# A maximum over 1024 keys in one VectorE instruction: two matmuls in a row, two banks freed together

## What is computed

```python
def attention(x, ctx, wq, wk, wv, wo, bo):        # self-attention: ctx is x
    q = x @ wq; k = ctx @ wk; v = ctx @ wv        # 16 heads of 64
    sim = einsum('bhid,bhjd->bhij', q, k) * 64 ** -0.5     # 1024 x 1024 per head
    attn = softmax(sim)
    return einsum('bhij,bhjd->bhid', attn, v) @ wo + bo
```

## Time and profile before

| | |
|---|---|
| median of 3 runs | 2324.59 us (2319.39 to 2327.59) |
| the profiled execution | 2328.06 us, its span 2326.3 us |
| TensorE busy | 2142.8 us, 92% |
| VectorE busy | 1743.6 us, 75% |
| ScalarE busy | 1476.1 us, 63% |
| GpSimd busy | 1155.2 us, 50% |

### The profile page before, as it was taken

The page is one execution under the profiler, slowest core; times in us unless marked ns, Lnnn a source line. Parts: engine busy times, 40 slices in busy tenths (PEclk is TensorE's granted clock), DMA queues, the critical chain, the costliest instruction groups (busy, mean ns, idle before and its releaser), DMA issues.

```text
span 2326.3 us, 59157 instructions
## 1 busy us (share of the span) xinstructions
PE 2142.8 (92%) x25392; PEld 1434.0 (62%) x25392; DVE 1743.6 (75%) x3148; ACT 1476.1 (63%) x1948; POOL 1155.2 (50%) x730
## 2 busy tenths in 40 slices
PE   4999999999899999989989999998998999999899
PEld 1566666675556666667556666666755666667675
DVE  5888888557588888755768888866576888886664
ACT  2788788345388888823547887773353888786342
POOL 3666665233076766622326766652223667664231
PEclk8999999999999999999999999999999999999999
DMA  3222221000132222001032222100103223210000
GB/s 107 71 73 52 61 62 38 10 31 23 51 105 52 58 74 63 18 10 38 24 83 73 52 75 77 43 27 1 38 23 81 70 61 83 61 36 20 10 11 19
DMA packets 60165, 114.19 MB, mean 49 GB/s; under 512 B 9344, under 2 KB 21632, under 8 KB 59904
## 3 DMA queue, kind: packets, MB, share of 16 engines
q1 hardware_dynamic: 59904, 110.41, 17.5%
HBM read 55.72 MB, written 4.19 MB: 26 GB/s over the span
## 4 chain that ended last, share of the span: by engine, by line
PE 65%; DVE 21%; ACT 9%; issue 3%; DMA 1%; POOL 1%; SPq 0%; POOLq 0%; DVEq 0%; ACTq 0%
PE scores L861 7%; DVE minima L1411 7%; PE scores L854 7%; PE work L831 7%; PE scores L746 6%; PE scores L748 6%; PE scores L747 6%; DVE prob L1426 4%; PE work L746 4%; PE work L747 4%; PE work L748 4%; PE work L883 3%; PE work L879 3%; PE work L881 3%; ACT prob L1214 3%
## 5 line engine op out<-in xcount | busy, mean ns | idle before, releaser
L693 POOL TENSOR_TENSOR prob<-prob 128x1024 f16<-128x1024 f32 x256 | 584.7, 2284 | 556.0 <-ACT prob L1215 545.2
L1411 DVE TENSOR_REDUCE minima<-work 128x1 f32<-128x512 f32 x1024 | 680.2, 684 | 43.0 <-PE work L831 29.4
L1214 ACT ACTIVATE prob<-scores 128x1024 f32<-128x1024 f32 x512 | 525.6, 1026 | 129.2 <-PE scores L861 112.0
L1215 ACT ACTIVATE prob<-scores 128x1024 f16<-128x1024 f32 x512 | 523.3, 1022 | 0.0
L883 PE MATMUL work<-vals,prob 128*128 128x65 f16 x4096 | 429.6, 196 | 0.0
L881 PE MATMUL work<-vals,prob 128*128 128x64 f16 x4096 | 429.4, 193 | 0.0
L879 PE MATMUL work<-vals,prob 128*128 128x65 f16 x4096 | 429.0, 193 | 0.4
L879 PEld LDWEIGHTS work<-vals,prob 128*128 128x128 f16 x4096 | 383.1, 99 | 62.1 <-issue 3.1
L881 PEld LDWEIGHTS work<-vals,prob 128*128 128x128 f16 x4096 | 379.9, 97 | 58.2
L831 PE MATMUL work<-ka,qa 128*128 128x512 f16 x1024 | 390.5, 386 | 24.0 <-DVE minima L1411 18.2
L883 PEld LDWEIGHTS work<-vals,prob 128*128 128x128 f16 x4096 | 380.3, 97 | 0.0
(11 more groups left out here) (160 smaller groups left out, 4179.0 us busy)
## 6 DMA issues: line engine op xcount, KB each, us to landing
qa<-staged_q SPq DMA_DIRECT2D x128, 128.0 KB, 2.3
ka<-staged_k SPq DMA_DIRECT2D x128, 128.0 KB, 2.3
raw_even<-in_pairs SPq DMA_DIRECT2D x32, 384.0 KB, 3.3
raw_odd<-in_pairs SPq DMA_DIRECT2D x32, 384.0 KB, 3.3
raw_odd<-in_pieces SPq DMA_DIRECT2D x20, 512.0 KB, 3.7
raw_even<-in_pieces SPq DMA_DIRECT2D x20, 512.0 KB, 3.6
qb<-staged_q SPq DMA_DIRECT2D x64, 128.0 KB, 2.3
kb<-staged_k SPq DMA_DIRECT2D x64, 128.0 KB, 2.3
```

The source lines that it names most:

```text
L693: pool.tensor_tensor(prob[1][:, slot, :], prob32[:, slot, :], prob[0][:, slot, :], ALU.subtract).then_inc(a.polished, 1)
L1214: act.activation(prob32[:, n % RING, :], source, ACT.Exp)
L1215: act.activation(prob[0][:, n % RING, :], source, ACT.Exp)\
L1411: dve.tensor_reduce(minima[:, t, h:h + 1], out[:, :], AX.X, ALU.max, negate=True)\
```

## The change

Both halves' matmuls of a tile stand in a row, into two neighbouring banks that are now one tile `peaks` of 1024 columns. One VectorE instruction reads all 1024 and writes the negated maximum, as float16, straight into the tile's column of `shift16`. The `combine` step, the tile `minima` and the semaphore `shift_combined` are gone. Both banks are filled and freed together, so the ring has one place: the next tile's first matmul waits until the read of this tile is over. `shift` writes into the same place, so it waits for tile 7's read, and the maximum behind it waits for the copy of `shift`. In the step list the maximum is now one entry, ahead of what is placed and of `score`.

```diff
-SCORE_RING, PEAK_RING, HIGH_RING = 2, 2, 1
+SCORE_RING, PEAK_RING, HIGH_RING = 2, 1, 1
...
-    tiles = [[Step("max", (t, h), par, head, 0) for h in range(BLKS)] for t in range(TILES)]
+    tiles = [[Step("max", t, par, head, 0)] for t in range(TILES)]
...
-    tiles[-1] = tiles[-1] + [Step("combine", 0, par, head, 0)]
...
-        out += [step for step in peaks_of[s] if step.kind == "arrive"] + peaks[:1]
+        out += peaks_of[s]
         out += placed[s]
         out.append(Step("score", s, par, head, 0))
         out += [take(step) for step in placed[s] if step.kind in HIGH]
-        out += peaks[1:] + [step for step in peaks_of[s] if step.kind == "combine"]
...
-        work = [ps(f"work{i}", BLK) for i in range(4)]
+        peaks = ps("peaks", 2 * BLK)
+        work = [peaks[:, 0:BLK], ps("work1", BLK), peaks[:, BLK:2 * BLK], ps("work3", BLK)]
...
-                    pe.wait_ge(a.peak_free, pace.n(*PEAK) + 1)
-                    return self_peaks[pace.here(*PEAK) % PEAK_RING]
+                    pe.wait_ge(a.peak_free, pace.n(*PEAK) + PEAK_RING)
...
-                        out = next_peak()
-                        t, h = s
-                        pe.matmul(out[:, :], qa[par][head][:, t * P:(t + 1) * P],
-                                  ka[par][head][:, h * BLK:(h + 1) * BLK], start=True, stop=True)\
-                            .then_inc(a.peak_full, 1)
+                        next_peak()
+                        for h in range(BLKS):
+                            last = pe.matmul(work[2 * h], qa[par][head][:, s * P:(s + 1) * P],
+                                             ka[par][head][:, h * BLK:(h + 1) * BLK], start=True, stop=True)
+                        last.then_inc(a.peak_full, 1)
...
-                        pe.wait_ge(a.shift_combined, pace.n("shift") + 1)
-                        pe.transpose(out[0:TILES, 0:P // 2].bitcast(F16), shift16[:, :], ident16[:, :])\
+                        pe.transpose(work[0][0:TILES, 0:P // 2].bitcast(F16), shift16[:, :], ident16[:, :])\
...
-                        dve.tensor_reduce(minima[:, t, h:h + 1], out[:, :], AX.X, ALU.max, negate=True)\
+                        dve.tensor_reduce(shift16[:, s:s + 1], peaks[:, :], AX.X, ALU.max, negate=True)\
                            .then_inc(a.peak_free, 1)
-                    elif step.kind == "combine":
-                        dve.wait_ge(a.peak_free, pace.n(*PEAK) + PEAK_RING)
-                        dve.tensor_reduce(shift16[:, :], minima[:, :, :], AX.X, ALU.min)\
-                           .then_inc(a.shift_combined, 1)
```

More of the change, by code:

```diff
@@ L215, in self_unit @@
     for s in range(TILES):
-        peaks = [step for step in peaks_of[s] if step.kind == "max"]
         if s == TILES - 1 and after:
             out.append(Step("shift", 0, *nxt, 0))
-        out += [step for step in peaks_of[s] if step.kind == "arrive"] + peaks[:1]
+        out += peaks_of[s]
         out += placed[s]
@@ L331, in build @@
         scores = [ps(f"scores{i}", 2 * BLK) for i in range(2)]
-        work = [ps(f"work{i}", BLK) for i in range(4)]
+        peaks = ps("peaks", 2 * BLK)
+        work = [peaks[:, 0:BLK], ps("work1", BLK), peaks[:, BLK:2 * BLK], ps("work3", BLK)]
         four = [scores[i][:, h * BLK:(h + 1) * BLK] for i in range(2) for h in range(2)]
         self_outs = work[3]
-        self_peaks = [work[0], work[2]]
         self_high = work[1]
@@ L1405, in do @@
                     elif step.kind == "max":
-                        out = next_peak()
-                        t, h = s
-                        if s == (0, 0) and pace.here("combine"):
-                            dve.wait_ge(a.shift_combined, pace.n("combine"))
-                        dve.tensor_reduce(minima[:, t, h:h + 1], out[:, :], AX.X, ALU.max, negate=True)\
+                        next_peak()
+                        dve.tensor_reduce(shift16[:, s:s + 1], peaks[:, :], AX.X, ALU.max, negate=True)\
                            .then_inc(a.peak_free, 1)
-                    elif step.kind == "combine":
-                        dve.wait_ge(a.peak_free, pace.n(*PEAK) + PEAK_RING)
-                        dve.tensor_reduce(shift16[:, :], minima[:, :, :], AX.X, ALU.min)\
-                           .then_inc(a.shift_combined, 1)
                     elif step.kind == "shift":
-                        out = next_peak()
+                        next_peak()
                         dve.wait_ge(a.row_ready, pace.n("shift", times=16) + CREDIT)
-                        dve.tensor_copy(shift_rows[:, :], out[0:TILES, 0:P // 2].bitcast(F16))\
+                        dve.tensor_copy(shift_rows[:, :], work[0][0:TILES, 0:P // 2].bitcast(F16))\
                            .then_inc(a.peak_free, 1)
```

7 lines of the change are left out of this document (3 added, 4 removed).

## The result

| | before | after |
|---|---|---|
| median | 2325.03 us, 4 runs (2319.39 to 2327.59) | 2369.97 us, 4 runs (2368.72 to 2373.04) |
| profiled execution's span | 2326.3 us | 2368.3 us |
| mean granted clock of TensorE | 0.990 | 0.983 |
| VectorE busy | 1743.6 us | 1737.3 us |

The ratio is 1.0199, 95% interval 1.0178 to 1.022. The forecast was 2336.6 us in a range of 2322 to 2351. The sign was right; the size was not: 45 us slower where 12 were expected.

The account below looks back on a forecast made before the run. TensorE, busy 92% of the span, was taken as the bound, with only its waits open to change. Pairs -3, round starts +8 and +7, clock +1.5 and DMA -1.5 gave +12 us: 2336.6 us, range 2322 to 2351.

Follow-up runs that it names:

- e2: The changed kernel with GpSimd's two scaling instructions of a weight split cut to 8 columns from the 31st split on: 2366.8 us, ratio 1.0187.
- e4: The changed kernel, but VectorE reads the single place in two halves and combines at the end: 2394.9 us, ratio 1.0308.
- e6: The changed kernel with all three GpSimd instructions of a weight split cut to 8 columns from the 31st split on: 2340.8 us, ratio 1.0073.
- e8: The changed kernel with a second place, idle score banks, for the first maxima of each round: 2333.7 us, ratio 1.0041.
- e3: The kernel before with both halves' maxima matmuls in a row, its two places and half reads kept: 2331.0 us, ratio 1.0033.
- e7: The changed kernel with VectorE's gather of key tile 3's value step moved behind the copy of the shift: 2345.6 us, ratio 1.0088.
- e9: The changed kernel with the gather behind the shift's copy and a second place for maxima at the starts of rounds: 2305.9 us, ratio 0.9914.
- e1: The kernel before with GpSimd's two scaling instructions of a weight split cut to 8 columns from the 31st split on: 2326.6 us, ratio 1.0012.
- e5: The kernel before with all three GpSimd instructions of a weight split cut to 8 columns from the 31st split on: 2318.2 us, ratio 0.9972.
- e10: e9 with GpSimd's split of W moved from step 3 to step 1 of a head-0 unit: 2295.2 us, ratio 0.9868.

## What to carry to other kernels

When a buffer of a ring is taken away or the order of an engine's work is changed, go over every instruction that stands ahead of the reader on its engine and ask two things. What is its *longest* duration in the trace, and is that hidden by the place that goes? A group whose mean is above its common duration (here 1366 against 1220 ns) says that such instructions are there. And what will the neighbouring engine be running when it starts at its new time? The second question can't be answered from the instruction's old duration: the refine ahead of key tile 5 was short before and became long by starting earlier. And keep the two parts of such a change apart: the merged read was worth 25 us, the lost place cost 64 (with half reads), and lending it a second place where one was free, with the gather moved behind the copy, made it 19 us faster than the kernel before.

## What the runs showed of the hardware

The refine on VectorE, both inputs in SBUF, stands behind a running GpSimd instruction and ends 1.07 to 1.09 us after that one's end, where it takes 1.22 us undisturbed; 937 refines in twelve kernels agree, and none was longer than 1.27 us otherwise. No list of waits shows it: the instruction is shown as longer. It works the other way too: the polish on GpSimd (L690), which takes 2.13 to 2.14 us alone, takes 2.80 where it starts beside a waiting or running refine (207.11 above). So GpSimd's work is not free for being on an engine that is idle half of the time: shortening one (e2) can move the next one under the refine and make it worse.

A VectorE reduction over two neighbouring PSUM banks costs as much per column as one over a single bank: 1223 ns for 1024 columns, 684 for 512, 635 for 462, about 1.05 ns a column and 0.15 us fixed.

The granted clock fell to its half level for 3.4 us at the end of many first units. Over the twelve profiled executions, by TensorE's idle time around the shift's transpose there: at 1.9 us or more (after, e2, e4, e6, e8) in 15 of 16 units, at 1.8 (e3, e7, e9) in 10 of 12, at 1.65 (before, e1, e5) in 1 of 8, and at 1.2 or less (e1, e2, e5, e6, e10) in none of 12. In e9 units with the same idle time of 1.8 us took 21.2 us without such a fall and 22.8 with it. So a wait that grows by 0.2 or 0.3 us can cost many times its growth, though not each time. Why the level falls 37 us behind a self-attention in one round and not in another stays open.
